# BF16 maximum rows first in the score sums, 32-column denominators, GpSimd's sum last, one maximum over two banks

## The chip, the cores and the metric

One core of one Trainium2 chip runs the whole kernel. The metric is the device time of one execution in microseconds (us). Engines are named as in the profile: PE is TensorE's matmuls, PEld its weight loads, DVE VectorE, ACT ScalarE, POOL GpSimd, SP SyncE, which issues the DMAs.

## The reference, cut to what matters

```python
x = x + attention(layernorm(x), W_qkv, W_out)     # x: 2 x 2048 x 256, 16 heads of 64
x = x + ffn(layernorm(x), ...)                    # one 256 x 256 product, low-rank part merged in

def attention(inputs, W_qkv, W_out):
    q, k, v = split(inputs @ W_qkv)
    score = einsum('bihd,bjhd->bijh', q, k) / 8
    wmat = softmax(causal(score), axis=2)
    return einsum('bijh,bjhd->bihd', wmat, v) @ W_out
```

## The kernel before, in words

There are three stages: the projection to q, k, v (to 314 us of the span), attention (to 1751 us) and the output projection with the feed-forward part. Attention works on 16 *items*, each a pair of heads with one batch element. The two heads lie on partitions 0 to 63 and 64 to 127, so the matmuls of a score sum come in pairs, one on each half of PE's rows, that run beside each other.

**Units.** An item has 4 query tiles t of 512 queries. A unit (t, j) is one block of 128 keys against the 512 queries of tile t; tile t has 4(t+1) units, an item 40. The last four units of a tile lie on the diagonal: they are narrower (512, 384, 256, 256 columns) and add a mask by four short BF16 matmuls (line 829). `score_unit` sums four terms in PSUM (line 822): q and k are each split in a high and a low fp32r part, which gives three pairs of matmuls, and the fourth pair subtracts the row maximum: `first_row` (a one in one row) times `shift` (the negated maxima, in one row for each head). ACT takes the exponential (line 948) into one of 8 buffers `probs`; two score buffers, so a unit's matmuls wait for the exponential two units before. `pv_unit` multiplies by v (line 886, fp32, four passes, which are two instructions each; output in 64 PE columns for each head). The exponentials are summed over keys by POOL (`sum_pool`, line 1123) for full units and by DVE (`sum_dve`, lines 1039 and 1049) for the last full unit and the diagonal; behind the second diagonal unit (d == 1) DVE adds `sum_pool` (line 1055). `denominators` then multiplies by ones (line 896, two fp32 matmuls in 64 columns), ACT copies the result, and by DMA it is spread, inverted by DVE and broadcast; POOL multiplies the output by it.

**Chunks.** The row maxima that an item subtracts are made beside the item before it: 40 chunks (16 query blocks against up to 4 key tiles) are matmuls of one high part pair each (line 850), into two banks of a ring of three PSUM banks, one for each head. DVE takes the maximum of each bank (line 1017). `ring_free` makes a chunk wait until the two banks that it takes have been read. The banks follow each other: (0,1), (2,0), (1,2) and so on, with one bank in between for a denominator or for the transposed maxima (`turn_max`). So a chunk always takes over the first bank of the chunk before it, if nothing lies between the two, and waits for that bank's maximum. After the last chunk the maxima are joined, transposed, copied (line 1029) and placed in `shift` by two DMAs (line 761), which the next item's first score unit waits for.

**Order on PE.** PE works through *blocks*, my name for one turn of the loop over s: block i is s = 2i. It has, in this order: chunks of slot 0, a score unit (two units ahead), chunks of slot 1, a score unit, chunks of slot 2, two pv units (2i and 2i+1), and at blocks 0, 2, 6 and 12 the denominators of the tile before. `plan_chunks` puts the chunks into the slots. DVE's order has chunks of slot 0 ahead of the addition of unit 2i, those of slots 1 and 2 ahead of that of unit 2i+1. The slots, with the chunk's width and its banks:

```
block      slot 0        slot 1        slot 2
 1                                     512 (1,2)
 2                       128 (0,1)     512 (2,0)   denominators 1
 3         512 (2,0)     512 (1,2)     512 (0,1)
 4         512 (2,0)                   256 (1,2)
 5         384 (0,1)                   512 (2,0)
 6                       128 (1,2)     512 (0,1)   denominators 2
 7         512 (0,1)     512 (2,0)     512 (1,2)
 8, 9      512 (0,1)     256, 384 (2,0) 512 (1,2)
10         512 (0,1)                   128 (2,0)
11         256 (1,2)                   512 (0,1)
12                       384 (2,0)     512 (1,2)   denominators 0
13         512 (1,2)     512 (0,1)     512 (2,0)
14,15,16   512 (1,2)     128, 256, 384 (0,1) 512 (2,0)
17         512 (1,2)                   turn 0
18, 19, 0  none; block 0: denominators 0
```

The last item has no chunks. In a block with a diagonal chunk or unit the short mask matmuls stand behind it (lines 858 and 829).

## Time and profile before

| | us |
|---|---|
| median of 3 runs (lowest, highest) | 1908.71 (1906.43, 1910.15) |
| the profiled execution, its time and its span | 1910.15, 1908.1 |
| attention: first and last exponential | 316.2, 1750.2 |
| PE busy, share of the span | 1833.8, 96% |
| DVE, POOL, ACT busy | 1272.3, 972.8, 806.7 |
| granted TensorE clock, mean | 0.991 |

A timeline row gives start, duration, engine, line, operation, output and inputs, shape and how many instructions are merged. A PE row starts when the first matmul is taken up, with the loading of its weights if that lies open. So the time that PE spends on something is best read from start to start of consecutive rows and not from the durations, which overlap. The trace shows waits of PE partly as idle time and partly as a longer distance from start to start.

### The profile page before, as it was taken

The page shows a single profiled execution, that of the slowest core. Times are in us where ns is not written, and L with a number is a line of the kernel's source. Part 1 is how long each engine was busy: PE and PEld are TensorE (multiplying, and loading weights), DVE is VectorE, ACT ScalarE, POOL GpSimd, SP SyncE. Part 2 cuts the span into 40 slices and gives each one's busy share as a digit, 9 for nine tenths or more (in the row PEclk, how much of TensorE's full clock was granted, in tenths as well). Part 3 has the DMA queues.
Part 4 walks back from the last instruction along what each step waited for, and adds up shares of the span by engine and source line. Part 5 has one row for each costly group of instructions (what it writes and reads, how often), then busy time and mean ns, then how long its engine had stood idle before and what let it go on. Part 6 is the DMA issues. An engine that isn't in the chain of part 4 may idle for free. (4 is left out here: it accounts for less than half of the span.)

```text
span 1908.1 us, 34290 instructions
## 1 busy us (share of the span) xinstructions
PE 1833.8 (96%) x13464; PEld 1128.0 (59%) x13464; DVE 1272.3 (67%) x2123; ACT 806.7 (42%) x982; POOL 972.8 (51%) x532
## 2 busy tenths in 40 slices
PE   7999998999999999999999999999999999998998
PEld 5877776555555555555555555555555555554897
DVE  5364652868676767676776767686777676747565
ACT  3222123454545454545454454545454545454221
POOL 1011000666675858575665666666758585746211
PEclk9999998999999999999999999999999999998999
DMA  5646445212121212222121312121212121023551
GB/s 204 223 179 232 164 157 210 68 35 78 41 73 46 72 46 68 62 58 67 46 74 51 80 45 79 40 74 46 67 46 73 46 68 51 24 73 102 177 192 56
DMA packets 150782, 171.33 MB, mean 90 GB/s; under 512 B 44618, under 2 KB 91744, under 8 KB 150624
## 3 DMA queue, kind: packets, MB, share of 16 engines
q1 hardware_dynamic: 150624, 169.15, 28.0%
q8 instruction: 108, 1.77, 0.4%
q14 instruction: 50, 0.41, 0.1%
HBM read 97.02 MB, written 71.57 MB: 88 GB/s over the span
## 5 line engine op out<-in xcount | busy, mean ns | idle before, releaser
L1017 DVE TENSOR_REDUCE f_part_max<-b_ring 128x1 f32<-128x512 f32 (+3 forms) x1200 | 675.3, 604 | 317.5 <-PE b_ring L850 213.5
L948 ACT ACTIVATE b_probs<-b_scores 128x1024 f32<-128x1024 f32 (+3 forms) x640 | 567.4, 898 | 615.5 <-PE b_scores L822 357.9
L1123 POOL TENSOR_TENSOR b_sum_pool<-b_sum_pool,b_probs 128x1024 f32<-128x1024 f32 x237 | 569.2, 2402 | 32.1 <-POOL b_sum_pool L1123 0.5
L1123 POOL TENSOR_TENSOR b_sum_pool<-b_probs 128x1024 f32<-128x1024 f32 x48 | 115.7, 2411 | 324.8 <-DVE g_sum_dve L1049 308.7
L822 PE MATMUL b_scores<-f_split 64*128 64x512 f32 (+2 forms) x1920 | 269.5, 383 | 9.1 <-ACT b_probs L948 7.3
L822 PE MATMUL b_scores<-b_split 64*128 64x512 f32 (+2 forms) x1920 | 268.0, 381 | 3.3 <-ACT b_probs L948 3.1
L886 PE MATMUL b_o_acc<-b_probs,f_v_in 128*64 128x512 f32 (+3 forms) x1280 | 270.5, 544 | 0.0
L886 PE MATMUL b_o_acc<-b_probs,b_v_in 128*64 128x512 f32 (+3 forms) x1280 | 269.0, 541 | 0.7 <-ACT b_probs L948 0.7
L1049 DVE TENSOR_TENSOR g_sum_dve<-g_sum_dve,b_probs 128x768 f32<-128x768 f32 (+3 forms) x243 | 229.5, 944 | 34.1 <-ACT b_probs L948 26.1
L822 PEld LDWEIGHTS b_scores<-b_split 64*128 64x128 f32 x1920 | 165.6, 185 | 51.0 <-issue 20.4
L822 PEld LDWEIGHTS b_scores<-f_split 64*128 64x128 f32 x1920 | 168.2, 187 | 46.0 <-issue 19.4
L346 DVE COPY a_stage_d<-a_made 128x512 f32<-128x512 f32 x96 | 66.1, 690 | 142.4 <-PE a_made L291 142.3
L850 PE MATMUL b_ring<-b_split 64*128 64x512 f32 (+2 forms) x640 | 141.8, 431 | 14.9 <-DVE f_part_max L1017 14.0
L346 ACT COPY a_stage_a<-a_made 128x512 f32<-128x512 f32 x96 | 56.5, 589 | 226.0 <-PE a_made L291 226.0
L886 PEld LDWEIGHTS b_o_acc<-b_probs,b_v_in 128*64 128x64 f32 x1280 | 77.6, 136 | 111.8 <-issue 93.0
L886 PEld LDWEIGHTS b_o_acc<-b_probs,f_v_in 128*64 128x64 f32 x1280 | 77.9, 136 | 110.2 <-issue 92.4
L850 PEld LDWEIGHTS b_ring<-b_split 64*128 64x128 f32 x640 | 64.6, 183 | 131.3 <-issue 126.3
L850 PE MATMUL b_ring<-f_split 64*128 64x512 f32 (+2 forms) x560 | 124.6, 432 | 10.9 <-DVE f_part_max L1017 9.9
L850 PEld LDWEIGHTS b_ring<-f_split 64*128 64x128 f32 x560 | 56.7, 183 | 112.7 <-issue 108.6
L822 PE MATMUL b_scores<-f_shift,p_first_row 64*128 64x512 f32 (+2 forms) x640 | 120.3, 364 | 0.0
L704 POOL TENSOR_TENSOR b_split<-f_raw,b_split 128x512 fp32r<-128x512 f32 x64 | 86.1, 1369 | 66.2 <-ACT b_split L934 66.2
L822 PE MATMUL b_scores<-b_shift,p_first_row 64*128 64x512 f32 (+2 forms) x640 | 119.4, 362 | 0.0
(135 smaller groups left out, 2288.5 us busy)
## 6 DMA issues: line engine op xcount, KB each, us to landing
f_raw<-k_t SPq DMA_DIRECT2D x32, 512.0 KB, 4.8
f_raw<-q_t SPq DMA_DIRECT2D x32, 512.0 KB, 5.6
g_recip<-r_t SPq DMA_DIRECT2D x128, 128.0 KB, 3.0
o_t<-g_o_norm SPq DMA_DIRECT2D x64, 256.0 KB, 2.0
q_t<-a_stage_a SPq DMA_DIRECT2D x32, 256.0 KB, 2.4
q_t<-a_stage_d SPq DMA_DIRECT2D x32, 256.0 KB, 2.0
k_t<-a_stage_a SPq DMA_DIRECT2D x32, 256.0 KB, 2.0
k_t<-a_stage_d SPq DMA_DIRECT2D x32, 256.0 KB, 2.0
```

The source lines that it names most:

```text
L346: copy(stage[e][s][:], made[:, g % BANKS, :]).then_inc(emptied[e], 1)
L704: vec.tensor_tensor(lo[u][:, cols], raw[p][:, which, inner], halves(hi[u][:, cols]), ALU.subtract).then_inc(split_lo, 1)
L822: last = nc.tensor.matmul(scores[s % 2][:, h, lo:TILE], lhs, b[u][head(h), queries], start=(term == 0), stop=(term == 3 and not diagonal))
L850: last = nc.tensor.matmul(rowwise[h][:, 0:wide], q_hi[u][head(h), ib * P:(ib + 1) * P], k_hi[u][head(h), c * TILE:c * TILE + wide], start= ...
L886: last = nc.tensor.matmul(o_acc[head(h), off:], v_in[u][:, j, head(h)], probs[s % PR][:, h, off:], start=(j == 0), stop=(j == NB * t + NB ...
L948: nc.scalar.activation(probs[s % PR][:, :, off:], scores[s % 2][:, :, off:], ACT.Exp, scale=scale).then_inc(exp_done, 1)
L1017: nc.vector.tensor_reduce(part_max[:, h, ib, c:c + 1], rowwise[h][:, 0:width], AX.X, ALU.max).then_inc(chunk_reduced, 1)
L1049: nc.vector.tensor_tensor(sum_dve[t % 2][:, :, off:], sum_dve[t % 2][:, :, off:], probs[s % PR][:, :, off:], ALU.add).then_inc(dve_added, 1)
L1123: nc.gpsimd.tensor_tensor(sum_pool[:], first, probs[s % PR][:], ALU.add).then_inc(pool_added, 1)
```

## The change

- The maxima are kept as two BF16 rows, the high part and the rest, in `max_high` and `max_low`; DVE makes them in two instructions, four DMAs place them. `first_rows` has ones in two rows for each head.
- In `score_unit` the pair with the maxima is now BF16 and comes first; chunks of slot 0 are issued between it and the three fp32r pairs. Chunks of slots 1 and 2 stand where they stood.
- The denominators are four matmuls of 32 PE columns and 256 queries instead of two of 64 and 512; ACT copies 256 columns, four DMAs spread them.
- DVE adds `sum_pool` behind the last diagonal unit (d == 3) instead of behind the second.
- Where a chunk's two banks are neighbours, (0,1) or (1,2), DVE takes both maxima in one instruction, which adds 2 to the semaphore at its end. That is so for 27 of the 40 chunks. The waits in `ring_free` are unchanged.
- In blocks 5 and 11 the narrow chunk moves from slot 0 to slot 1.
- The high part of the output weights gets a buffer of its own, and the last tile's denominators in the third stage are changed like the others (both not shown).

```diff
@@ -526,7 +531,7 @@
             elif s == nb * t:
                 want = "B.s" if t else "..."
             else:
-                want = "s.B" if t else "..B"
+                want = ".sB" if t else "..B"
             pools = {"B": big, "s": small, ".": None}
             plan.append([[pools[w].pop(0)] if pools[w] else [] for w in want])
     assert not big and not small, (len(big), len(small))
...
@@ -729,8 +735,9 @@
                 def invert(n, t):
 
                     wait_apart(sp, den_copied, n * TI + t + 2, o_stored, 1)
-                    for h in range(2):
-                        sp.dma_start(den_spread[:, h, :], den_row[h * D:h * D + 1, :].rearrange(
+                    for c in range(4):
+                        h, half = divmod(c, 2)
+                        sp.dma_start(den_spread[half * D:(half + 1) * D, h, :], den_row[c * P // 4:c * P // 4 + 1, :].rearrange(
                             "o (p i) -> o p i", i=NB)).then_inc(den_moved, 16)
 
                     wait_apart(sp, inverted, n * TI + t + 1, o_stored, 1)
...
@@ -816,11 +824,16 @@
                     queries = slice(t * TILE + lo, (t + 1) * TILE)
                     keys = slice(j * P, (j + 1) * P)
                     diagonal = j >= NB * t
-                    for term, (a, b) in enumerate(((k_hi, q_hi), (k_hi, q_lo), (k_lo, q_hi), (None, shift))):
+                    for h in range(2):
+                        nc.tensor.matmul(scores[s % 2][:, h, lo:TILE], consts["first_rows"][head(h), :],
+                                         shift[u][head(h), queries], start=True, stop=False)
+                    for k in between:
+                        chunk(n + 1, 1 - u, k)
+                    for term, (a, b) in enumerate(((k_hi, q_hi), (k_hi, q_lo), (k_lo, q_hi))):
                         for h in range(2):
-                            lhs = consts["first_row"][head(h), :] if a is None else a[u][head(h), keys]
-                            last = nc.tensor.matmul(scores[s % 2][:, h, lo:TILE], lhs, b[u][head(h), queries],
-                                                    start=(term == 0), stop=(term == 3 and not diagonal))
+                            last = nc.tensor.matmul(scores[s % 2][:, h, lo:TILE], a[u][head(h), keys],
+                                                    b[u][head(h), queries], start=False,
+                                                    stop=(term == 2 and not diagonal))
                     if diagonal:
                         for side in range(2):
                             cols = slice(off + side * D, off + (side + 1) * D)
...
@@ -892,21 +905,24 @@
                     pe.wait_ge(dve_added, sum_ready[n, t])
                     ring_free(now, before)
                     denom = ring[:, ring_banks["denom", t][0], :]
-                    for h in range(2):
-                        last = nc.tensor.matmul(denom[head(h), :], consts["ones"][:, 0:D],
-                                                sum_dve[t % 2][:, h, :], start=True, stop=True)
+                    for c in range(4):
+                        h, half = divmod(c, 2)
+                        cols = slice(half * DEN, (half + 1) * DEN)
+                        last = nc.tensor.matmul(denom[c * P // 4:(c + 1) * P // 4, 0:DEN], consts["ones"][:, 0:P // 4],
+                                                sum_dve[t % 2][:, h, cols], start=True, stop=True)
                     last.then_inc(denom_made, 1)
 
                 def item(pair, u, following, previous=True):
                     n = pair * 2 + u
                     for s in range(0, U, 2):
                         places = plan[s // 2] if following else ((), (), ())
+                        assert s + AHEAD < U or not any(places)
                         for e in range(2):
-                            for k in places[e]:
-                                chunk(n + 1, 1 - u, k)
                             ahead = s + e + AHEAD
                             if ahead < U:
-                                score_unit(n, u, ahead)
+                                for k in places[1] if e else ():
+                                    chunk(n + 1, 1 - u, k)
+                                score_unit(n, u, ahead, () if e else places[0])
                             elif following:
                                 score_unit(n + 1, 1 - u, ahead - U)
                         for k in places[2]:
...
@@ -1008,13 +1024,18 @@
 
             @block.vector
             def _(dve):
-                def reduce_chunk(m, k, rowwise, turn):
+                def reduce_chunk(m, k, banks, turn):
                     ib, c = chunks[k]
                     width = min(TILE, (ib + 1) * P - c * TILE)
 
                     dve.wait_ge(chunk_made, m * CH + turn + 1)
+                    first, second = banks
+                    if second == first + 1:
+                        nc.vector.tensor_reduce(part_max[:, :, ib, c], ring[:, first:second + 1, 0:width], AX.X,
+                                                ALU.max).then_inc(chunk_reduced, 2)
+                        return
                     for h in range(2):
-                        nc.vector.tensor_reduce(part_max[:, h, ib, c:c + 1], rowwise[h][:, 0:width], AX.X,
+                        nc.vector.tensor_reduce(part_max[:, h, ib, c:c + 1], ring[:, banks[h], 0:width], AX.X,
                                                 ALU.max).then_inc(chunk_reduced, 1)
 
                 def finish_max(m):
...
@@ -1026,8 +1047,10 @@
                 def take_rows(m):
 
                     dve.wait_ge(max_turned, m + 1)
-                    nc.vector.tensor_copy(max_rows[:], ring[:, ring_banks["turn", 0][0], 0:P]
-                                          ).then_inc(max_rows_ready, 1)
+                    turned = ring[:, ring_banks["turn", 0][0], 0:P]
+                    nc.vector.tensor_copy(max_high[:], turned).then_inc(lead["max_high_ready"], 1)
+                    dve.wait_ge(lead["max_high_ready"], m + 1)
+                    nc.vector.tensor_tensor(max_low[:], turned, max_high[:], ALU.subtract).then_inc(max_rows_ready, 1)
 
                 def add_unit(n, s):
                     t, j = units[s]
...
@@ -1048,7 +1071,7 @@
                     dve.wait_ge(dve_added, dve_before[n, s])
                     nc.vector.tensor_tensor(sum_dve[t % 2][:, :, off:], sum_dve[t % 2][:, :, off:], probs[s % PR][:, :, off:],
                                             ALU.add).then_inc(dve_added, 1)
-                    if d == 1 and first_dve(n, t) < NB * t:
+                    if d == NB - 1 and first_dve(n, t) < NB * t:
 
                         dve.wait_ge(dve_added, dve_before[n, s] + 1)
                         dve.wait_ge(pool_added, pool_done[n, t])
...
```

## Rows read from the trace of the kernel before

**Rows 1.** The page's first part, busy time of each engine

```profile
PE 1833.8 (96%) x13464; PEld 1128.0 (59%) x13464; DVE 1272.3 (67%) x2123; ACT 806.7 (42%) x982; POOL 972.8 (51%) x532
```

**Rows 2.** The tile f_max_rows: ns min/median/max, first and last start

```profile
L1029 DVE CAST f_max_rows<-b_ring x15: 290/292/293, 406.6 to 1666.1; 128x128 fp32r<-128x128 f32 x15
L761 SPq DMA_DIRECT2D f_shift<-f_max_rows x14: 550/564/791, 496.7 to 1577.2; - x14
...
DMA to landing us min/median/max: 1.8/1.8/2.8
```

**Rows 3.** Waits in total: who <- for whom, us, times, longest

```profile
PEld b_ring L850 <- issue: 234.9, 364, 1.5
...
PE b_ring L850 <- DVE f_part_max L1017: 23.9, 51, 0.9
```

**Rows 4.** PE's timeline, blocks 13 and 14: start us, us, what

```profile
1014.50 0.50 PE L850 MATMUL b_ring<-f_split 64*128 64x512 f32 x2
...
1015.87 0.50 PE L850 MATMUL b_ring<-f_split 64*128 64x512 f32 x2
...
1018.17 0.50 PE L850 MATMUL b_ring<-f_split 64*128 64x512 f32 x2
1018.51 0.86 PE L822 MATMUL b_scores<-b_split 64*128 64x512 f32 x6
1019.21 0.39 PE L822 MATMUL b_scores<-b_shift,p_first_row 64*128 64x512 f32 x2
1019.55 0.39 PE L850 MATMUL b_ring<-f_split 64*128 64x256 f32 x2
...
1020.83 0.42 PE L850 MATMUL b_ring<-f_split 64*128 64x512 f32 x2
...
1023.04 0.50 PE L850 MATMUL b_ring<-f_split 64*128 64x512 f32 x2
```

**Rows 5.** DVE's timeline of block 14

```profile
1018.72 1.82 DVE L1017 TENSOR_REDUCE f_part_max<-b_ring 128x1 f32<-128x512 f32 x4 [1.02 <-PE b_ring L850]
1021.28 1.29 DVE L1017 TENSOR_REDUCE f_part_max<-b_ring 128x1 f32<-128x512 f32 x2 [0.75 <-PE b_ring L850]
```

**Rows 6.** Groups by line and form: xcount, busy us, mean ns, idle before

```profile
L1017 DVE TENSOR_REDUCE f_part_max<-b_ring 128x1 f32<-128x512 f32 x840 | 540.6, 685 | 295.5 <-PE b_ring L850 213.5 <-PE b_ring L858 74.2
...
L447 DVE TENSOR_REDUCE f_part_max<-a_rowwise 128x2 f32<-128x1024 f32 x28 | 34.1, 1216 | 0.0
...
L447 DVE TENSOR_REDUCE f_part_max<-a_rowwise 128x2 f32<-128x768 f32 x4 | 3.8, 949 | 0.0
...
L822 PEld LDWEIGHTS b_scores<-b_split 64*128 64x128 f32 x1920 | 165.6, 185 | 51.0 <-issue 20.4 <-ACT b_probs L948 18.0
...
L829 PEld LDWEIGHTS b_scores<-p_pick,p_late_keys 64*128 64x128 bf16 x1024 | 30.9, 95 | 32.3 <-issue 22.7
```

**Rows 7.** PE's timeline, block 2 and the denominators behind it

```profile
961.15 0.97 PE L822 MATMUL b_scores<-b_split 64*128 64x512 f32 x6
961.95 0.40 PE L822 MATMUL b_scores<-b_shift,p_first_row 64*128 64x512 f32 x2
...
962.38 0.94 PE L822 MATMUL b_scores<-b_split 64*128 64x512 f32 x6
963.15 0.39 PE L822 MATMUL b_scores<-b_shift,p_first_row 64*128 64x512 f32 x2
...
965.48 1.03 PE L896 MATMUL b_ring<-g_sum_dve,p_ones 128*64 128x512 f32 x4
966.44 0.50 PE L850 MATMUL b_ring<-f_split 64*128 64x512 f32 x2
```

**Rows 8.** The timeline of all engines, block 5

```profile
976.50 1.23 DVE L1055 TENSOR_TENSOR g_sum_dve<-g_sum_dve,b_sum_pool 128x1024 f32<-128x1024 f32 x1
...
977.76 0.97 DVE L1017 TENSOR_REDUCE f_part_max<-b_ring 128x1 f32<-128x384 f32 x2
...
978.41 0.49 PE L850 MATMUL b_ring<-f_split 64*128 64x512 f32 x2 [0.54 <-DVE f_part_max L1017]
```

More of the change, by code:

```diff
@@ L233, in place_first_max @@
                     for h in range(2):
-                        sp.dma_start(halves(shift[h * D:h * D + 1, :]).rearrange("o (b i) -> o b i", i=P),
-                                     halves(max_rows[h * KB:(h + 1) * KB, :])).then_inc(lead["max_placed"], 16)
+                        for i, rows in enumerate((max_high, max_low)):
+                            sp.dma_start(shift[h * D + i:h * D + i + 1, :].rearrange("o (b i) -> o b i", i=P),
+                                         rows[h * KB:(h + 1) * KB, :]).then_inc(lead["max_placed"], 16)
                 def tile(T, u, ahead):
@@ L660, in attention @@
         k_hi, k_lo, q_hi, q_lo = ([split[u][:, i, :] for u in range(2)] for i in range(4))
-        shift = [lead["shift"], sb("shift1", [P, L], F32R)]
+        shift = [lead["shift"], sb("shift1", [P, L], BF16)]
         v_in = [lead["v_in"], sb("v_in1", [P, KB, P])]
@@ L804, in _, with score_unit @@
             def _(pe):
-                def score_unit(n, u, s):
+                def score_unit(n, u, s, between=()):
                     t, j = units[s]
@@ L1082, in item @@
                             for k in here:
-                                reduce_chunk(n + 1, k, [ring[:, bank, :] for bank in ring_banks["chunk", k]],
-                                             turn_of[k])
+                                reduce_chunk(n + 1, k, ring_banks["chunk", k], turn_of[k])
                         if following and s == 2 * LAST_CHUNK_PAIR:
@@ L1338, in _ @@
                 pe.wait_ge(tail["dve_added"], tail["dve_ops"])
-                for h in range(2):
-                    half = slice(h * P // 2, (h + 1) * P // 2)
-                    last = nc.tensor.matmul(last_denom[half, :], consts["ones"][:, 0:P // 2],
-                                            tail["sum_dve"][last_t % 2][:, h, :], start=True, stop=True)
+                for c in range(4):
+                    h, half = divmod(c, 2)
+                    cols = slice(half * DEN, (half + 1) * DEN)
+                    last = nc.tensor.matmul(last_denom[c * P // 4:(c + 1) * P // 4, :], consts["ones"][:, 0:P // 4],
+                                            tail["sum_dve"][last_t % 2][:, h, cols], start=True, stop=True)
                 last.then_inc(tail["denom_made"], 1)
@@ L1490, in attend @@
             "split": sb("split", [P, 4, length], F32R),
-            "shift": sb("shift", [P, length], F32R),
+            "shift": sb("shift", [P, length], BF16),
             "v_in": sb("v_in", [P, length // P, P]),
```

61 lines of the change are left out of this document (35 added, 26 removed).

## The prediction

> **What bounds the kernel now.** I read the busy times first. The reader is to see that PE is busy for 96% of the span and no other engine for more than 67% [rows 1], so a microsecond saved on PE can count, and one saved on DVE counts only where PE waits for DVE. Attention is 16 items; the first and the last of the 15 copies of the maxima are 1259.5 us apart, so an item takes 1259.5 / 14 = 89.96 us [rows 2]. The waits of the chunks are hard to see in the view of waits: it puts 234.9 us before the chunks' weights down to "issue" and only 23.9 us to DVE's maximum [rows 3]. The timelines tell more. In block 14 PE starts a chunk at 1018.17 and the next at 1019.55. DVE starts the first maximum at 1018.72 [rows 5], 0.55 later, and one bank of 512 takes 0.685 [rows 6]: the first bank is read at 1019.405, and PE goes on 0.145 later. Block 13 is alike, 1.37 between its chunks at 1014.50 and 1015.87 [rows 4]. Without the wait the way is shorter: three fp32r pairs take 1019.21 - 1018.51 = 0.70, 0.233 each, so chunk (0.34), three pairs (0.70) and the maxima's pair (0.23) are 1.27 [rows 4]. So PE here already runs at the release of a chunk's *first* bank: the ring of three banks makes every chunk take over the first bank of the one before.
>
> **One maximum over two banks.** One instruction of 2 x 512 takes 1.216, of 2 x 384 0.949 (the same operation in the first stage), against 0.685 for one bank of 512 [rows 6]; 2 x 256 are as many elements as that, and I take 0.685 for them. DVE gains little: two banks one behind the other last 1.29 [rows 5], so 0.07. But the first bank is now free after 1.216 instead of 0.685, 0.53 later, and nothing in PE's order gives that back. Rather the opposite: with the maxima's pair ahead of the chunk, only three pairs (0.70) are left between the chunk of slot 0 and that of slot 1.
>
> Block 14 before: chunks at 0, 1.38 and 2.66, next block at 4.87 [rows 4]. After: maxima's pair 0.235, chunk of slot 0 at 0.235 with its weights loaded ahead, DVE starts 0.45 behind it (as 1020.83 to 1021.28, a chunk without open weights [rows 4, 5]), 1.216, and 0.145 to PE: slot 1 at 2.05, where PE would be ready at 0.235 + 0.233 + 0.70 = 1.17. That is 0.67 later than before. Behind the chunk of slot 1 the way to slot 2 is about 0.07 shorter (BF16 weights), and 0.02 at pv: block 14 is 0.58 longer. The same sum, with the widths of its chunks, for the others of this kind:
> - blocks 7, 8, 9: slot 0 merged, slot 1 not: +0.67, +0.58, +0.66.
> - block 13: slot 1 is merged too and 512 wide, so slot 2 waits 0.55 + 1.216 + 0.145 = 1.91 behind it instead of 1.37 [rows 4]: +0.67 + 0.54 = +1.21.
> - blocks 15 and 16: slot 1 merged, 256 and 384 wide: 0.5 + 0.685 + 0.145 = 1.33 and 0.55 + 0.949 + 0.145 = 1.65 to slot 2 instead of about 1.27 and 1.33: +0.75 and +0.99.
> - block 3: slot 0 not merged (1.51 instead of 1.37), slot 1 merged (+0.53): +0.67.
>
> Together 0.58 + 1.91 + 1.21 + 1.74 + 0.67 = +6.11 us an item.
>
> **Blocks behind a diagonal.** In block 5 DVE adds `sum_pool` for 1.23 at 976.50 ahead of the chunk's maximum at 977.76, and PE's next chunk waits until 978.41 [rows 8]. That addition goes behind the last diagonal unit, and the narrow chunk comes a slot later, behind one more addition (about 0.68). What is late next is still DVE: blocks 4 and 5 gain 0.15, blocks 10 and 11 0.28. But the addition then stands ahead of the maxima of blocks 6 and 12, so the chunk of slot 2 there waits: DVE is done with its additions about 2.2 behind the block's start, the narrow maximum (0.4 to 0.55) and 0.145 follow, slot 2 comes at 2.7 instead of 2.25, and with its weights open (0.1): +0.49 and +0.53. Sum +0.59. Bounds: nothing, if DVE keeps up, less 2.0 if all four stalls of these blocks go; +1.5 if each of blocks 5 and 11 loses as well.
>
> **Denominators.** Before, 965.48 to 966.44 = 0.96: twice 0.43 and 0.10 to the next kind of tile [rows 7]. Four strips of 32 columns side by side, with half the columns each, are 0.43, with a change of tile ahead of it and one behind 0.63: -0.33, four times an item, -1.32. Bounds: 0.43 and one change (-0.43) up to four strips one after another, 4 x 0.43 + 0.2 = 1.92 (+0.96). I take the value near the row, where two strips of 64 already run side by side. *The Trainium skill, "TensorEngine Tiling (Array Packing)", section Tiling Modes, says that a change of the tiling mode, not only of the tile, drains the engine. The 0.10 at 966.44 agrees with it; by this rule pv (64 columns) to denominators (32 columns) is a change that the kernel before did not have, which is the second 0.10 in my 0.63; without the rule the sum would be 6 us less over 64 tiles.*
>
> **The maxima's pair first and in BF16.** Where PE comes from pv or from a wait, the first weight load lies open: score and shift start 0.80 apart at 961.15 against 0.70, and behind a BF16 mask 0.77 [rows 7]. A BF16 load lasts 95 ns instead of 185 [rows 6], so about 0.09 of the 0.10 goes, and where it is not open the pair is some 0.015 shorter. Counted in the blocks without waits, 18, 19, 0, 1 and 2: -0.18, -0.11, -0.10, -0.14, -0.22, together -0.75 (between 0 and -1.5). In block 0 what comes ahead of the second unit is lost again, since that waits for ACT. Block 17 stays as it is: the transposed maxima wait for DVE. In all other blocks this gain is in the sums above. The maxima reach `shift` later: a second DVE instruction of 0.29 and two more DMAs of 0.57 on SP's queue, 1.5 us with the wait between; before, the copy, two DMAs and 1.8 to landing are 0.29 + 1.14 + 1.8 = 3.2 [rows 2]. PE asks for them two pv units and block 18 later, by the pairs above some 1.9 + 3.0 = 4.9, so 4.7 is just in time and I cost it at nothing; with a landing of 2.8 [rows 2] PE would wait 0.9 an item. SP's two more DMAs for the denominators, 1.1 us, lie ahead of DVE's reciprocals, which stand at fixed places two blocks and more later.
>
> **The sum.** An item with chunks: 6.11 + 0.59 - 1.32 - 0.75 = +4.6 us; 15 of them +69.5. The last item has no chunks: 20 blocks of pairs of units at -0.14 to -0.18 and four denominators give -4.9. The first and last stage: -0.3. The profiled execution took 1910.15, which is 1.4 above the median: 1910.15 + 69.5 - 5.2 = 1974.5, and by the median 1973. I forecast **1974 us, slower**.
>
> **Rivals.**
>
> A, *the ring's wait is not DVE's*: the view of waits calls most of it "issue" [rows 3]; then PE's own queue makes these gaps, a bank that is free later costs nothing, and the gains stand alone: -1.32 for denominators, about -3.2 for weights in all blocks, -2.0 for the stalls behind diagonals, -6.5 an item, some 1808 us. It decides as soon as slot 1 comes at about 1.2 and not at 2.05 in block 14. Against it stands the constant 0.145 behind the first bank's end, whatever comes before. With what lies between it and 1905 it has 0.15.
>
> B, *strips of 32 columns do not overlap as I take it*: two at a time, 0.96 + 0.10 instead of 0.63, 64 x 0.43 = +27: 2001 us; all one after another 2057. For it: the trace has no such tile. Chance 0.08.
>
> C, *waits and gains are both there, but the waits are half as long*, since PE takes up other work or DVE starts earlier: +3.0 for the first sum instead of 6.1: 1928 us. Chance 0.10.
>
> D, *no change*, both sums equal within 0.2%: 0.04, which leaves 0.63 for the forecast.
>
> **How the numbers follow.** The forecast's own range is 1955 to 1995 (1.3 us an item). With C below and the smaller case of B above I give 1925 to 2003. Between 1905 and 1913 (0.2% is about what a measurement of this kernel can tell from no change) lies 0.04; faster 0.15, slower 0.81.
>
> **What would show it.** In the timeline of blocks 7 to 9 and 13 to 16, the chunk of slot 1 starts some 0.14 behind the end of a 1.2 us maximum, about 1.8 behind the chunk of slot 0, and PE is idle before it; the copies of the maxima lie about 94.6 us apart; the denominators take 0.63 from start to start; in block 5 the maximum of the narrow chunk no longer stands behind `sum_pool`. Wrong would be the forecast if the slot 1 chunks start at 1.2 to 1.4 of their block, or if an item takes less than 90 us.

## The result, and the profile after

| | before | after |
|---|---|---|
| median, us (lowest, highest; runs) | 1908.74 (1906.43, 1910.15; 4) | 1995.62 (1993.81, 1996.44; 4) |
| profiled execution, span | 1908.1 | 1994.3 |
| after / before | | 1.0452, 95% interval 1.0439 to 1.0465 |
| one item with chunks, us | 89.96 | 95.86 |

The changed kernel is slower by 86.9 us, 4.5%. The forecast was 1974 with a range of 1925 to 2003.

The busy times, to hold against [rows 1]: PE is busy for 45 us less than before, since its work became less, and the span grew by 86.2.

```profile
PE 1788.7 (90%) x13720; PEld 1056.1 (53%) x13720; DVE 1245.7 (62%) x1734; ACT 791.4 (40%) x982; POOL 964.3 (48%) x532
```

The copies of the maxima, two now, of [rows 2]. The first is at 411.9 and the fifteenth at 1754.0, so an item takes 1342.1 / 14 = 95.86 us.

```profile
L1051 DVE CAST f_max_high<-b_ring x15: 290/291/292, 411.9 to 1754.0; 128x128 bf16<-128x128 f32 x15
L1053 DVE TENSOR_TENSOR f_max_low<-b_ring,f_max_high x15: 291/291/292, 412.2 to 1754.3; 128x128 bf16<-128x128 f32 x15
```

The view of waits, to hold against [rows 3] (who <- for whom: us, times, longest). The weights' "issue" is as before; new is that PE is idle for 137 us ahead of chunks for line 1034, the maximum over two banks, where it was idle for 24 for DVE's maxima.

```profile
PEld b_ring L863 <- issue: 245.4, 305, 2.1
...
PE b_ring L863 <- DVE f_part_max L1034: 137.0, 197, 1.7
```

Block 14 of the same item on PE, to hold against [rows 4] (start us, us, engine, line, operation). The block starts at 1062.39, the chunk of slot 1 comes at 1064.50, that of slot 2 at 1065.68, the next block at 1067.94. So slot 1 comes 2.11 behind the start of the block, where it was 1.38, and the 0.79 of idle time ahead of it are put down to line 1034.

```profile
1062.39 0.39 PE L828 MATMUL b_scores<-b_shift,p_first_rows 64*128 64x512 bf16 x2
1062.43 0.59 PE L863 MATMUL b_ring<-f_split 64*128 64x512 f32 x2
1062.86 0.86 PE L834 MATMUL b_scores<-b_split 64*128 64x512 f32 x6
1064.50 0.39 PE L863 MATMUL b_ring<-f_split 64*128 64x256 f32 x2 [0.79 <-DVE f_part_max L1034]
...
1065.68 0.46 PE L863 MATMUL b_ring<-f_split 64*128 64x512 f32 x2
...
1067.94 0.39 PE L828 MATMUL b_scores<-b_shift,p_first_rows 64*128 64x512 bf16 x2
```

DVE in blocks 13 and 14, to hold against [rows 5]. The merged maximum of block 14 starts at 1063.13 and ends at 1064.36; PE goes on 0.14 later.

```profile
1056.74 1.23 DVE L1034 TENSOR_REDUCE f_part_max<-b_ring 128x2 f32<-128x1024 f32 x1 [1.77 <-PE b_ring L863]
1058.72 1.23 DVE L1034 TENSOR_REDUCE f_part_max<-b_ring 128x2 f32<-128x1024 f32 x1 [0.75 <-PE b_ring L863]
1060.63 1.29 DVE L1038 TENSOR_REDUCE f_part_max<-b_ring 128x1 f32<-128x512 f32 x2 [0.69 <-PE b_ring L863]
1063.13 1.23 DVE L1034 TENSOR_REDUCE f_part_max<-b_ring 128x2 f32<-128x1024 f32 x1 [1.21 <-PE b_ring L863]
1065.07 0.43 DVE L1034 TENSOR_REDUCE f_part_max<-b_ring 128x2 f32<-128x256 f32 x1 [0.71 <-PE b_ring L871]
```

Groups by form, to hold against [rows 6] (times, busy us, mean ns, idle before).

```profile
L1034 DVE TENSOR_REDUCE f_part_max<-b_ring 128x2 f32<-128x1024 f32 x285 | 349.4, 1226 | 275.1 <-PE b_ring L863 206.8 <-PE b_ring L871 67.9
...
L1038 DVE TENSOR_REDUCE f_part_max<-b_ring 128x1 f32<-128x512 f32 x270 | 173.8, 685 | 99.2 <-PE b_ring L863 95.7 <-PE b_ring L871 3.5
...
L828 PEld LDWEIGHTS b_scores<-f_shift,p_first_rows 64*128 64x128 bf16 x640 | 33.0, 94 | 110.5 <-issue 95.1 <-ACT b_probs L964 12.4
```

The denominators, to hold against [rows 7]. From 1005.53 to 1006.10 they take 0.57, where they took 0.96.

```profile
1003.66 1.94 PE L899 MATMUL b_o_acc<-b_probs,b_v_in 128*64 128x512 f32 x8
1005.53 0.64 PE L911 MATMUL b_ring<-g_sum_dve,p_ones 128*32 128x256 f32 x8
1006.10 0.39 PE L828 MATMUL b_scores<-b_shift,p_first_rows 64*128 64x512 bf16 x2
```

Blocks 5 and 6 on all engines, to hold against [rows 8]. The reader is to see three things: the reciprocal at 1017.26 waits for its DMA and stands ahead of the narrow maximum at 1017.95; PE's chunk of slot 2 waits until 1019.05; in block 6 `sum_pool` (line 1078) now stands at 1021.24, ahead of the narrow maximum at 1022.38, and the chunk at 1022.95 waits for that.

```profile
1013.64 2.40 SPq L740 DMA_DIRECT2D g_den_spread<-g_den_row  x4
...
1015.98 0.94 DVE L1072 TENSOR_TENSOR g_sum_dve<-g_sum_dve,b_probs 128x768 f32<-128x768 f32 x1
...
1017.26 0.20 DVE L1098 RECIPROCAL g_recip_spread<-g_den_spread 128x8 f32<-128x8 f32 x1 [0.35 <-DMA g_den_spread<-g_den_row]
1017.39 0.65 DVE L1072 TENSOR_TENSOR g_sum_dve<-g_sum_dve,b_probs 128x512 f32<-128x512 f32 x1
...
1017.95 0.95 DVE L1034 TENSOR_REDUCE f_part_max<-b_ring 128x2 f32<-128x768 f32 x1
...
1019.05 0.49 PE L863 MATMUL b_ring<-f_split 64*128 64x512 f32 x2 [1.41 <-DVE f_part_max L1034]
...
1021.24 1.22 DVE L1078 TENSOR_TENSOR g_sum_dve<-g_sum_dve,b_sum_pool 128x1024 f32<-128x1024 f32 x1
...
1022.38 0.42 DVE L1034 TENSOR_REDUCE f_part_max<-b_ring 128x2 f32<-128x256 f32 x1
...
1022.95 0.50 PE L863 MATMUL b_ring<-f_split 64*128 64x512 f32 x2 [0.46 <-DVE f_part_max L1034]
```

**Block by block.** From the start of a block to the start of the next, in us. A row is the sum of the medians of its blocks over 14 items; "mean" is the change of the mean over the same items; "forecast" is the prediction's own change. The means add up to the change of a real item (95.86 - 89.97), the medians need not.

| blocks | before | after | change | mean | forecast |
|---|---|---|---|---|---|
| 18, 19, 0, 1, 2 (with two denominators) | 18.77 | 17.53 | -1.24 | -1.09 | -1.41 |
| 3 | 5.05 | 5.77 | +0.72 | +0.72 | +0.67 |
| 4 and 5 | 8.29 | 8.50 | +0.21 | -0.17 | -0.15 |
| 6 (with denominators) | 5.28 | 5.53 | +0.25 | +0.25 | +0.16 |
| 7, 8, 9 | 14.93 | 17.03 | +2.10 | +2.09 | +1.91 |
| 10 and 11 | 7.91 | 7.51 | -0.40 | -0.33 | -0.28 |
| 12 (with denominators) | 5.35 | 5.67 | +0.32 | +0.32 | +0.20 |
| 13 | 5.05 | 6.38 | +1.33 | +1.32 | +1.21 |
| 14, 15, 16 | 14.70 | 17.48 | +2.78 | +2.80 | +2.32 |
| 17 | 4.56 | 4.54 | -0.02 | -0.03 | 0 |
| item | 89.89 | 95.93 | +6.04 | +5.89 | +4.64 |
| last item, without chunks | 82.91 | 82.16 | -0.75 | (one item) | -4.9 |

Medians and means disagree in blocks 4 and 5. Block 4 is 0.49 shorter in the mean. Block 5 has two kinds of durations in the changed kernel, 4.04 to 4.17 in six of the 14 items and 4.68 to 5.38 in the other eight, and a median shows one of them alone.

### The profile page after: what moved, and what is told of

The parts are those of the page before. It is cut to its first block and busy times, and to the rows that moved or that the text cites. A ratio compares the mean times of both kernels' runs of the same rounds, so it can differ in the third digit from the quotient of the medians.

```text
span 1994.3 us, 34978 instructions
## 1 busy us (share of the span) xinstructions
PE 1788.7 (90%) x13720; PEld 1056.1 (53%) x13720; DVE 1245.7 (62%) x1734; ACT 791.4 (40%) x982; POOL 964.3 (48%) x532
## 5 line engine op out<-in xcount | busy, mean ns | idle before, releaser
L1034 DVE TENSOR_REDUCE f_part_max<-b_ring 128x2 f32<-128x1024 f32 (+3 forms) x405 | 428.1, 1057 | 320.2 <-PE b_ring L863 206.8
L1038 DVE TENSOR_REDUCE f_part_max<-b_ring 128x1 f32<-128x512 f32 (+3 forms) x390 | 222.8, 613 | 119.3 <-PE b_ring L863 95.7
L834 PE MATMUL b_scores<-b_split 64*128 64x512 f32 (+2 forms) x1920 | 285.2, 405 | 0.0
L834 PE MATMUL b_scores<-f_split 64*128 64x512 f32 (+2 forms) x1920 | 285.0, 403 | 0.0
L1072 DVE TENSOR_TENSOR g_sum_dve<-g_sum_dve,b_probs 128x768 f32<-128x768 f32 (+3 forms) x243 | 219.1, 901 | 35.6 <-ACT b_probs L964 26.0
L863 PE MATMUL b_ring<-b_split 64*128 64x512 f32 (+2 forms) x640 | 149.5, 455 | 77.0 <-DVE f_part_max L1034 71.0
L834 PEld LDWEIGHTS b_scores<-f_split 64*128 64x128 f32 x1920 | 177.5, 188 | 15.4
L834 PEld LDWEIGHTS b_scores<-b_split 64*128 64x128 f32 x1920 | 177.0, 188 | 15.4
L828 PE MATMUL b_scores<-f_shift,p_first_rows 64*128 64x512 bf16 (+2 forms) x640 | 117.4, 357 | 12.3 <-ACT b_probs L964 10.2
L828 PE MATMUL b_scores<-b_shift,p_first_rows 64*128 64x512 bf16 (+2 forms) x640 | 117.1, 357 | 5.7 <-ACT b_probs L964 4.7
```

The lines of the kernel that those rows point to most:

```text
L828: nc.tensor.matmul(scores[s % 2][:, h, lo:TILE], consts["first_rows"][head(h), :], shift[u][head(h), queries], start=True, stop=False)
L834: last = nc.tensor.matmul(scores[s % 2][:, h, lo:TILE], a[u][head(h), keys], b[u][head(h), queries], start=False, stop=(term == 2 and not ...
L863: last = nc.tensor.matmul(rowwise[h][:, 0:wide], q_hi[u][head(h), ib * P:(ib + 1) * P], k_hi[u][head(h), c * TILE:c * TILE + wide], start= ...
L1034: nc.vector.tensor_reduce(part_max[:, :, ib, c], ring[:, first:second + 1, 0:width], AX.X, ALU.max).then_inc(chunk_reduced, 2)
L1038: nc.vector.tensor_reduce(part_max[:, h, ib, c:c + 1], ring[:, banks[h], 0:width], AX.X, ALU.max).then_inc(chunk_reduced, 1)
L1072: nc.vector.tensor_tensor(sum_dve[t % 2][:, :, off:], sum_dve[t % 2][:, :, off:], probs[s % PR][:, :, off:], ALU.add).then_inc(dve_added, 1)
```

## The experiments

Each run shared its chip with runs of the kernel before; the ratio is to those. e1 to e4 and e11 ran on one chip, e5 to e8 on a second, e9 and e10 on a third, so runs of different chips are compared by their ratios. "Item" is the sum of the blocks' medians, "mean item" the mean over 14 items (kernel before: 89.89 and 89.97). Three of the eleven expected ranges held, those of e5, e6 and e11.

| run | us | ratio to before, 95% interval | item | mean item |
|---|---|---|---|---|
| e1 changed, two maxima again | 1908.85 | 1.0003 (0.9994 to 1.0013) | 89.83 | 90.21 |
| e2 before, merged maximum alone | 1997.26 | 1.0471 (1.0453 to 1.0488) | 95.58 | 95.71 |
| e3 before, banks given back late | 2032.3 | 1.0653 (1.0635 to 1.0671) | 98.25 | 98.17 |
| e4 = e1, chunk ahead of the BF16 pair | 1904.2 | 0.9978 (0.9966 to 0.9991) | 89.37 | 89.72 |
| e5 = e4, `sum_pool` early, old slots | 1882.39 | 0.9863 (0.9846 to 0.9879) | 88.13 | 88.27 |
| e6 = e5, two DMAs for the denominators | 1878.46 | 0.9842 (0.9826 to 0.9858) | 88.14 | 88.24 |
| e7 before, `sum_pool` last and new slots alone | 1915.05 | 1.0033 (1.0022 to 1.0043) | 90.46 | 90.37 |
| e8 before, denominators alone | 1895.66 | 0.9928 (0.9911 to 0.9944) | 89.12 | 89.28 |
| e9 = e6, merged where nobody waits | 1876.69 | 0.9828 (0.9815 to 0.9842) | 87.83 | 88.06 |
| e10 = e9, narrow chunk inside the unit | 1874.6 | 0.9818 (0.9804 to 0.9831) | 87.67 | 87.82 |
| e11 = e4, two DMAs for the denominators | 1892.67 | 0.9910 (0.9894 to 0.9927) | 89.10 | 89.24 |

**e1: the merged maximum undone.**

```diff
-                    if second == first + 1:
+                    if False:
```

> The changed kernel with one thing undone: each chunk's two banks are read by two maxima again (all else as changed). My theory (a merged maximum gives the first bank back 0.53 us later and PE waits for just that): nearly the whole loss goes. Slot 1 of blocks 7 to 9 and 13 to 16 comes 1.5 us behind the block's start instead of 2.05, slot 2 of block 13 1.37 behind slot 1 instead of 1.9; an item takes about 88 us, the kernel 1870 to 1900 us, faster than before. Rival A (the gaps ahead of chunks are PE's own queue, and the loss comes from the new order or the BF16 pair): it stays near 1990. Rival E (the loss is from the sum of POOL being added last, ahead of the maxima of blocks 6 and 12): most of it stays, since only blocks 6 and 12 would hold it.

Measured 1908.85: the whole loss goes, and no more. Rival A is out, and so is rival E as the cause of the loss. PE and DVE in block 14:

```profile
1023.22 0.39 PE L828 MATMUL b_scores<-b_shift,p_first_rows 64*128 64x512 bf16 x2
1023.25 0.58 PE L863 MATMUL b_ring<-f_split 64*128 64x512 f32 x2
...
1024.72 0.39 PE L863 MATMUL b_ring<-f_split 64*128 64x256 f32 x2 [0.19 <-DVE f_part_max L1038]
...
1025.91 0.41 PE L863 MATMUL b_ring<-f_split 64*128 64x512 f32 x2
```

```profile
1023.88 2.09 DVE L1038 TENSOR_REDUCE f_part_max<-b_ring 128x1 f32<-128x512 f32 x4 [1.03 <-PE b_ring L863]
```

Slot 1 comes 1.50 behind the start of the block, as expected; 1023.88 + 0.685 + 0.155 is 1024.72. But the time was expected at 1870 to 1900 and is not below that of before, so this expectation failed: the other parts of the change together bring nothing. Where their gains went is what e4 to e8 and e11 are for.

**e2: the merged maximum alone.** In `reduce_chunk` of the kernel before:

```diff
+                    first, second = ring_banks["chunk", k]
+                    if second == first + 1:
+                        nc.vector.tensor_reduce(part_max[:, :, ib, c], ring[:, first:second + 1, 0:width], AX.X,
+                                                ALU.max).then_inc(chunk_reduced, 2)
+                        return
```

> The kernel before with the merged maximum alone. My theory: slot 1 of blocks 7 to 9 and 13 to 16 0.53 us later, slot 2 of blocks 3 and 13 too, something behind the diagonals; about 5 us an item, 1975 to 1990 us. Rival A: DVE has 27 x 0.07 us less to do an item, the time stays at 1909 or falls a little. If the loss needs the new order as well (three pairs and not four between the chunks), it is clearly under 40 us.

Measured +4.7%, 88 us, 7 us above the range. The new order isn't needed for it. Blocks 7, 8, 9 and 14 are each 0.61 longer and block 13 1.21. Of the 0.61, 1.23 - 0.69 = 0.54 is the longer maximum; the other 0.07 is that it starts 0.62 behind the chunk's start, where one over a single bank starts 0.55 behind ([rows 4, 5] and e3 below). One place gains: block 11 is 0.44 shorter, since DVE has less to do there. Block 14:

```profile
1061.21 0.50 PE L850 MATMUL b_ring<-f_split 64*128 64x512 f32 x2
...
1063.20 0.39 PE L850 MATMUL b_ring<-f_split 64*128 64x256 f32 x2 [0.56 <-DVE f_part_max L1018]
...
1064.47 0.43 PE L850 MATMUL b_ring<-f_split 64*128 64x512 f32 x2
```

```profile
1061.83 1.23 DVE L1018 TENSOR_REDUCE f_part_max<-b_ring 128x2 f32<-128x1024 f32 x1 [1.09 <-PE b_ring L850]
```

The maximum ends at 1063.06 and PE goes on at 1063.20.

**e3: the same instructions as before, the bank given back late.** In `ring_free`:

```diff
-                            pe.wait_ge(chunk_reduced, (n + 1 + back) * 2 * CH + 2 * turn_of[which] + i + 1)
+                            pe.wait_ge(chunk_reduced, (n + 1 + back) * 2 * CH + 2 * turn_of[which] + 2)
```

> The kernel before, two maxima as before, but a chunk that takes over a bank waits until both banks of that older chunk are read, and not only the one that it takes. No instruction changes its form. My theory (only the moment of release counts): a wait of 0.6 us more at slot 1 of all full blocks and at slot 2 where slot 1 is 512 wide (blocks 3, 7, 13), 6 to 8 us an item, 2000 to 2030 us. A rival by which the merged instruction itself is costly (a slower read over two banks, or a later start) leaves it at 1909.

Measured 2032.3, 2 us above the range. This is the cleanest of the runs: nothing but the number that a wait compares with is changed, and 123 us come. In blocks 13 to 16, where the chunks that PE waits for are merged in e2, the two agree block for block: block 13 +1.21 and +1.19, 14 +0.61 and +0.60, 15 +0.81 and +0.80, 16 +1.07 and +1.06. So in these blocks the merged instruction isn't costly by itself; it is costly because it gives both banks back at its end. In block 14 two maxima start at 1080.33 and last 1.29 together, and the chunk that only takes over the first one's bank comes at 1081.76, 0.14 behind the second:

```profile
1079.78 0.50 PE L850 MATMUL b_ring<-f_split 64*128 64x512 f32 x2
...
1081.76 0.39 PE L850 MATMUL b_ring<-f_split 64*128 64x256 f32 x2 [0.55 <-DVE f_part_max L1017]
...
1083.03 0.43 PE L850 MATMUL b_ring<-f_split 64*128 64x512 f32 x2
```

```profile
1080.33 1.29 DVE L1017 TENSOR_REDUCE f_part_max<-b_ring 128x1 f32<-128x512 f32 x2 [1.02 <-PE b_ring L850]
```

**e4: the chunk of slot 0 ahead of the whole unit.**

```diff
-                                for k in places[1] if e else ():
-                                    chunk(n + 1, 1 - u, k)
-                                score_unit(n, u, ahead, () if e else places[0])
+                                for k in places[e]:
+                                    chunk(n + 1, 1 - u, k)
+                                score_unit(n, u, ahead)
```

> As e1, with the chunk of slot 0 ahead of the whole score unit again, so that four pairs lie between slot 0 and slot 1. My theory: slot 1 of seven blocks comes at 1.38 and not at 1.54, blocks 4 and 10 pay 0.1 for open fp32r weights: 1 us an item less than e1, 15 us, 1855 to 1885 us. A rival by which a chunk behind the BF16 pair is cheaper (its weights loaded beside that pair): 5 to 15 us slower than e1.

1904.2 against 1908.85, 4.7 us less where 15 were expected (1855 to 1885). The blocks do as the theory says: 3, 7 to 9 and 13 to 17 are each 0.12 to 0.13 shorter. But block 10 takes 0.37 more, and block 18 0.36 more, where PE waits for the maxima to be placed: in e4 the last DMA of the maxima lands 3.0 to 3.7 behind the start of block 18, once 4.4, and block 19 starts 0.09 later. So the order "maxima's pair, chunk, rest" costs 0.12 in the blocks that wait for a bank.

**e5: `sum_pool` early again.** This is e4 with the line in `add_unit`, the two lines that count DVE's additions (not shown) and the slots put back:

```diff
-                    if d == NB - 1 and first_dve(n, t) < NB * t:
+                    if d == 1 and first_dve(n, t) < NB * t:
...
-                want = ".sB" if t else "..B"
+                want = "s.B" if t else "..B"
```

> As e4 (two maxima, chunk first), and GpSimd's sum is added behind the second diagonal unit again, with the narrow chunks of blocks 5 and 11 back in slot 0. What is left of the change: the BF16 pair first, 32-column denominators. Theory F (the gains of e1 were eaten behind the diagonals, since the additions of DVE now stand ahead of the maxima that slot 2 of blocks 5, 6, 11 and 12 waits for): blocks 5, 6, 11 and 12 together 2 us shorter than in e4, an item 87 to 88 us, 1870 to 1885 us. Rival G (the gains were eaten by the four DMAs for the denominators, for which DVE's reciprocal waits in blocks 5 and 9): blocks 5 and 11 keep their 0.6, the time stays above 1890.

1882.39, inside theory F's range and below the 1890 of rival G: by the means blocks 5, 6, 11 and 12 together are 2.6 shorter than in e4. How much of it G can claim all the same is for e11. Blocks 4 and 10 take back 1.4 and block 18 gives another 0.3.

**e6: two DMAs instead of four for the denominators.** The edit to e5, without the counts in the waits and the same lines of the third stage:

```diff
-                    for c in range(4):
-                        h, half = divmod(c, 2)
-                        sp.dma_start(den_spread[half * D:(half + 1) * D, h, :], den_row[c * P // 4:c * P // 4 + 1, :].rearrange(
+                    for h in range(2):
+                        sp.dma_start(den_spread[:, h, :], den_row[h * D:(h + 1) * D:P // 4, :].rearrange(
                             "o (p i) -> o p i", i=NB)).then_inc(den_moved, 16)
```

> As e5, with the denominators spread by two DMAs (one for each head, its source two partitions) instead of four. By theory F DVE's reciprocal comes without a wait and little lies on the path: 0 to 5 us less than e5. By rival G most of the rest of the loss goes here: 15 us or more below e5.

4 us less than e5 on the same chip. The medians of all blocks are those of e5 within 0.03; what is less lies in single items and in the last one (80.75 for 81.66). The intervals of the two ratios overlap, though all four runs of e6 lie below all four of e5; I take this as likely and not as shown. With `sum_pool` early little of the wait lies on PE's path.

**e7: `sum_pool` last and the new slots, on the kernel before.** The two counts are not shown.

```diff
-                    if d == 1 and first_dve(n, t) < NB * t:
+                    if d == NB - 1 and first_dve(n, t) < NB * t:
...
-                want = "s.B" if t else "..B"
+                want = ".sB" if t else "..B"
```

> The kernel before with only GpSimd's sum added last and the narrow chunks of blocks 5 and 11 in slot 1. Theory F: block 4 and 10 end earlier, blocks 5, 6, 11 and 12 later, 1 to 2 us more an item, 1922 to 1940 us. By my forecast's step (4 and 5: -0.15, 10 and 11: -0.28, 6 +0.49, 12 +0.53) +0.6 an item: 1918. Rival G: no change, 1909, or faster.

+6.5 us, clear of rival G's "no change" (the interval of the ratio is above 1), but less than theory F's range, 1922 to 1940, and than what my forecast's step gives (+0.6 an item). An item shows +0.57 by the medians and +0.40 in the mean, and 15 times 0.40 is near the 6.5. By the medians blocks 4 and 10 give 0.37 and 0.47 back, 6 and 12 lose 0.41 and 0.61, 11 loses 0.55. In block 12 the reader sees why: the addition of `sum_pool` at 1011.54 and the narrow maximum behind it, whose first half (0.55) is over at 1013.23, then PE's chunk at 1013.38.

```profile
1011.09 0.41 DVE L1049 TENSOR_TENSOR g_sum_dve<-g_sum_dve,b_probs 128x256 f32<-128x256 f32 x1
1011.54 1.23 DVE L1055 TENSOR_TENSOR g_sum_dve<-g_sum_dve,b_sum_pool 128x1024 f32<-128x1024 f32 x1
1012.68 1.01 DVE L1017 TENSOR_REDUCE f_part_max<-b_ring 128x1 f32<-128x384 f32 x2
```

```profile
1011.60 0.34 PE L850 MATMUL b_ring<-f_split 64*128 64x384 f32 x2
...
1013.38 0.50 PE L850 MATMUL b_ring<-f_split 64*128 64x512 f32 x2 [0.36 <-DVE f_part_max L1017]
```

**e8: 32-column denominators alone.** The matmuls; the four DMAs, the copy and the third stage follow as in the change (not shown).

```diff
+                    for c in range(4):
+                        h, half = divmod(c, 2)
+                        cols = slice(half * DEN, (half + 1) * DEN)
+                        last = nc.tensor.matmul(denom[c * P // 4:(c + 1) * P // 4, 0:DEN], consts["ones"][:, 0:P // 4],
+                                                sum_dve[t % 2][:, h, cols], start=True, stop=True)
```

> The kernel before with only the 32-column denominators and their four DMAs. Each of the 63 tiles costs PE 0.57 instead of 0.96, as in the changed kernel: -0.39 x 63 = -25 us, if nothing waits for the DMAs: 1884. With DVE waiting for the two more DMAs (0.3 to 0.5 in blocks 5 or 9, where PE waits for DVE): up to 8 us of that are lost, 1884 to 1892 us. Rival G: 1900 or more.

-12.9 us, half of the expected, and between the ranges of my theory (to 1892) and of rival G (1900 and more). My number for a tile was wrong: 0.57 instead of 0.96 leaves out that pv now ends with a change of tile as well, 0.10. Blocks 0, 2, 6 and 12 are 0.28 to 0.29 shorter each, which is 1.15 an item. Of that, 0.28 and 0.08 come back in blocks 10 and 4. What makes block 10 longer I have not settled; PE's order in it runs as before up to the pv units (at 1.87 in both), and the time is lost behind that.

**e9 and e10: the best mixture.** In e9, which is e6 otherwise, `merged` holds the chunks of slot 2 and those of slot 0 in blocks 10 and 11 (its definition is not shown); in e10 the narrow chunk of slot 1 in blocks 8, 9 and 14 to 16 is issued behind the second unit's BF16 pair.

```diff
-                    if False:
+                    if second == first + 1 and k in merged:
...
-                                for k in places[e]:
-                                    chunk(n + 1, 1 - u, k)
-                                score_unit(n, u, ahead)
+                                inner = [k for k in places[e] if e and s in (16, 18, 28, 30, 32) and min(TILE, (chunks[k][0] + 1) * P - chunks[k][1] * TILE) < TILE]
+                                for k in places[e]:
+                                    if k not in inner:
+                                        chunk(n + 1, 1 - u, k)
+                                score_unit(n, u, ahead, inner)
```

> As e6, and the maximum is merged over two banks only where no chunk takes the first bank over within 1.9 us: the neighbouring chunks of slot 2, and slot 0 of blocks 10 and 11 (11 of 40 chunks). If only the moment of release counts, these merges cost nothing and DVE's 0.07 for each helps where it is late: in e2 blocks 10 and 11 were 0.43 shorter. 1870 to 1876 us. Rival H (a merged maximum costs PE something even where nobody waits for the bank): 1880 or more.

> As e9, and in blocks 8, 9, 14, 15 and 16 the narrow chunk of slot 1 is issued inside the second score unit, behind its BF16 pair, so that five pairs and not four lie between it and the chunk whose bank it takes. My theory: its wait of 0.12 goes and slot 2, asked for 0.2 earlier, waits little since a narrow maximum is short: 0.05 to 0.15 less for each of the five blocks, 1862 to 1872 us. Rival H or a wait that only moves to slot 2: as e9 within 3 us.

1876.69, 0.7 above e9's range, and 1874.6, 2.6 above e10's. e9 is 0.3 an item below e6: blocks 4 and 5 together -0.07, 10 and 11 together -0.24, the others as they were. So a merged maximum costs nothing where nobody waits for its first bank. Its 0.9828 can't be told from e6's 0.9842. e10 gains 0.12 in block 14 and 0.02 in 8 and 15, and loses 0.01 to 0.02 in 9 and 16, where the wait moves to slot 2: less than expected, and within the noise of e9, as the rival has it by which the wait only moves. e10 is the fastest of all, 0.9818 (0.9804 to 0.9831), 35 us below the kernel before.

**e11: why `sum_pool` last costs 22 us and not 6.5.** e4 with e6's edit.

> As e4 (GpSimd's sum last, narrow chunks in slot 1, chunk first, two maxima), with two DMAs instead of four for the denominators. GpSimd's sum last cost 6.5 us on the kernel before (e7) and 22 us in company (e4 against e5). If the other 15 us are DVE's wait for the two more DMAs in block 5, which stands ahead of the narrow maximum there, this run comes to 1887 to 1893 us. If they are DVE's additions alone, which a shorter block leaves less time for, it stays at 1899 to 1904 us.

0.9910 against e4's 0.9978, some 13 us. DVE's wait for the spread denominators falls with it, from 30 times to 12 (the waits of the last item, which are most of the microseconds, stay). The first line is e4's, the second e11's:

```profile
DVE g_recip_spread L1098 <- DMA g_den_spread<-g_den_row: 44.6, 30, 10.9
```

```profile
DVE g_recip_spread L1097 <- DMA g_den_spread<-g_den_row: 30.0, 12, 10.8
```

The time is in the expected range, but the 13 us are not all the DMAs' share of the 22, since two DMAs also save some 4 us where `sum_pool` is early (e6 against e5). The four runs make a square:

| ratio to before | four DMAs | two DMAs | saved by two |
|---|---|---|---|
| `sum_pool` last, new slots | 0.9978 (e4) | 0.9910 (e11) | 13 us |
| `sum_pool` early, old slots | 0.9863 (e5) | 0.9842 (e6) | 4 us |
| cost of `sum_pool` last | 22 us | 13 us | |

So `sum_pool` last costs 13 us with two DMAs, and about 9 of the 22 hang on the DMAs, give or take some 6 us by the four intervals. The 13 are twice the 6.5 of e7. Part of the rest is in block 18, which waits for the placed maxima: in the mean 3.36 in e11 and 2.99 in e6. I have not separated that from DVE's additions. Block 5 alone is 0.27 shorter in e11 than in e4 in the median and 0.64 in the mean; single items waited 1 to 2 us there.

## Why the prediction was right, point by point

**What bounds it.** Right. The view of waits says "issue" for most of the time ahead of a chunk, and e3, in which only a number in a wait differs, shows that it is DVE's release. Where PE is idle for a maximum ahead of a chunk, it goes on 0.145 to 0.148 behind its end in the trace of every kernel here. Rival A, with a chance of 0.15, is out by this and by e2.

**One maximum over two banks.** Right in mechanism, a bit small in size. Block 14 was forecast at +0.58 and has +0.66; 7, 8 and 9 +2.10 for 1.91; 13 +1.33 for 1.21. Block 14 was to bring slot 1 at 0.235 + 0.45 + 1.216 + 0.145 = 2.05, and it came at 0.04 + 0.70 + 1.23 + 0.14 = 2.11: the chunk is taken up right behind the maxima's pair (1062.43) and read 0.70 later (1063.13), of which 0.07 belongs to the merged form (0.63 in e1). Blocks 15 and 16 were the largest miss, +0.93 and +1.20 for +0.75 and +0.99: slot 1 comes 0.06 late as in block 14, slot 2 follows 1.40 and 1.73 behind it for 1.33 and 1.65, since its merged maximum starts 0.57 and 0.62 behind slot 1 and not 0.50 and 0.55, and pv follows slot 2 some 0.07 later than before. Undone alone (e1) or done alone (e2) the merge is worth 87 and 88 us. The whole loss of the change is this part.

**Behind the diagonals.** The forecast had +0.59 an item without the denominators. Measured alone (e7) it is +0.40 in the mean and +0.57 by the medians. In the changed kernel blocks 4 and 5 are 0.17 shorter in the mean, for a forecast of 0.15. One step behind this is nevertheless wrong: "SP's two more DMAs for the denominators, 1.1 us, lie ahead of DVE's reciprocals, which stand at fixed places two blocks and more later". The place is fixed, but SP issues them late: for tile 0 the first DMA goes out 6 to 7 us behind ACT's copy, since SP waits for the output of the tile before. Before, the spread denominators of tile 0 landed 1 to 2.5 us ahead of the reciprocal; two more DMAs at 0.59 and shorter blocks use that up. In the changed kernel DVE waits at tile 0's reciprocal in nine items, which adds up to 3.6 us, so this step costs little there. Without the merged maxima it costs more: with `sum_pool` last, two DMAs in place of four save 13 us (e11 against e4).

**Denominators.** 0.63 a tile was forecast, with one change of tile on each side. The four strips do run side by side. The two pv units ahead of them take 1.87 (1003.66 to 1005.53), 0.10 more than without a change of tile behind them, and the denominators 0.57: 0.29 less in all, as blocks 0, 2, 6 and 12 of e8 show too, for 0.33 forecast. So the second change of tile is there, 0.10 at each side; the four strips themselves take 0.04 more than half of the two before. Rival B, with a chance of 0.08, is out. The Trainium skill ("TensorEngine Tiling (Array Packing)", section Tiling Modes) says that changing the tiling mode drains the engine; the trace agrees, with 0.10 for each change.

**The maxima's pair first, in BF16.** A block's first unit after pv is 0.12 shorter, a unit behind a mask 0.08 to 0.10 and one elsewhere 0.01, near what the forecast took; the difference of e8 and e5 is 13 us. The split over the blocks was less good: by the medians of e5 against e8, 0.21 in block 19 and 0.02 in block 0, for 0.11 and 0.10. The placed maxima were said to be just in time, and are: in ten of 14 items of the changed kernel they land 2.5 to 2.6 behind the start of block 18 and are asked for at 2.85; in the other four SP is later and they cost 0.1 to 0.7 each, 1.6 us together, which the forecast put at nothing.

**The last item.** -4.9 was forecast, -0.75 measured. Each of its plain blocks is shorter, by 0.08 to 0.20, as forecast; but it has waits that I did not look at. DVE stands still there four times, 27 us in all, for the spread denominators (26 before), and PE's denominators wait for DVE's sum. Time gained ahead of such a wait can be lost at it: at block 6 PE is idle for 2.7 for that sum, where it was 0.6, and the block is 1.5 longer. Block 13 is 1.5 longer as well, and for that I have no cause.

**The sum.** Forecast +69.5 and -5.2; measured +88.0 for the 15 items with chunks, -0.75 for the last and -1 for what lies around them, 86.2 of span. The forecast is 22 us short: 4 at the last item, and 1.2 an item. By the means, 0.82 of that are in the blocks with merged maxima (3, 7 to 9, 13 to 16), 0.32 in blocks 18 to 2, where denominators and BF16 pair bring less than forecast, and 0.21 in blocks 6 and 12. The term that was too small is the first: +6.11 an item, measured +6.93. Rival C, by which it was to be 3.0, is out.

**How right.** The way and the mechanism were forecast; the size was 22 us low, a quarter of the whole loss. The forecast's own range was 1955 to 1995, and 1995.6 lies just above it. The stated range reached up to 2003 only because the smaller case of rival B, 2001, was let in, and that case did not occur. So the measured time lies in the stated range by some luck.

**The ledger by the runs.** Starting from before at 1908.7: denominators -13 (e8), BF16 pair first -13 (e5 against e8), `sum_pool` last with its slots and the waits that it meets +22 (e4 against e5), the chunk behind the pair +5 (e1 against e4), the merged maximum +87. The first four add up to nothing, which is why e1 lands on the kernel before. The terms hold in this order: `sum_pool` last alone is +6.5, with two DMAs +13 and with four +22.

## What to carry to other kernels

With a ring of few buffers, ask at each instruction that reads one *when the next user of its first part may go on*; joining two reads into one made the reader's own work 0.06 us shorter (1.29 to 1.23) and let the next user go on 0.61 us later (e2). A joined read is free where nobody waits for its first part (e9). To find such a wait, measure the constant between the end of the reader and the next start of the user in the timeline; the view of waits may name nobody. An addition that is moved off one path goes onto another: name the instruction that is queued behind it in its new place. And where a duration has two values, compare means and not medians.

## What the runs showed of the hardware

- A change from 64-column to 32-column strips costs PE 0.10 us, as one from columns to row halves does (e8 against before: the denominators start 0.10 later in blocks 0 and 2, with the same pv units ahead); four strips of 32 columns by 256 run side by side in fp32, 0.57 with the change behind them against 0.96 for two of 64 by 512.
- A maximum over two PSUM banks starts 0.07 us later behind the matmul that it waits for than one over a single bank: 0.62 against 0.55 (e2, e3), 0.70 against 0.63 (changed kernel, e1).
- Behind a BF16 pair that comes fresh from pv, the next fp32r pair is taken up only 0.04 later and the one behind that 0.42 to 0.43 later (1062.39, 1062.43, 1062.86): the trace books the open fp32r weight load to the second pair, and a block's first unit of 512 columns is 0.12 shorter all the same (0.92 to 0.93 for 1.03 to 1.04, e5 and e8).
- A DMA may read two partitions 32 apart and write 128 partitions in one issue of 0.56 us (e6), where two of 0.59 did the same work in e5.
